# q and k made once per token group, attention scores for two heads at a time, identity products left out, and a new step order, in a one-core transformer kernel

## What is computed

```python
x = x + 0.5 * ffn(_layernorm(x))       # fp4-rounded FFN, inner width 352
x = x + mamba(_layernorm(x))           # 2 layers, 256 channels, 16 states each
x = x + 0.5 * ffn(_layernorm(x))
x = x + 0.5 * moe(_layernorm(x))       # 8 experts, hidden width 512
x = x + attn(_layernorm(x))            # 16 heads of 8, bias by distance, causal
x = x + 0.5 * moe(_layernorm(x))

# attn
xn = _layernorm(x, ln_gamma, ln_beta)
q = proj(Wq) / math.sqrt(DH); k = proj(Wk); v = proj(Wv)
scores = jnp.einsum('bhid,bhjd->bhij', q, k) + rel[:, dist]
attn = jax.nn.softmax(jnp.where(causal, scores, -inf), axis=-1)
return x0 + jnp.einsum('bhij,bhjd->bhid', attn, v).reshape(B, T, D) @ Wo.T
```

## Time and profile before

| | |
|---|---|
| median of 3 runs | 2702.1 us (2699.7 to 2704.14) |
| the profiled execution | 2699.89 us |
| its span from first to last instruction | 2698.1 us |
| mean granted TensorE clock | 0.969 of full |
| instructions | 41593 |

### The profile page before, as it was taken

One profiled execution on the slowest core, in us unless ns is written; L12 is line 12 of the kernel. 1 busy time (PEld: TensorE's weight loads), 2 busy tenths in 40 slices (PEclk: granted clock), 3 DMA queues, 4 the chain that ended last, 5 costly groups with the idle time before them and its releaser, 6 DMA issues.

```text
span 2698.1 us, 41593 instructions
## 1 busy us (share of the span) xinstructions
PE 2506.0 (93%) x14781; PEld 1756.5 (65%) x14781; DVE 1943.5 (72%) x3913; ACT 1612.1 (60%) x3465; POOL 1367.7 (51%) x1227
## 2 busy tenths in 40 slices
PE   7999999997898999887899999998999999999988
PEld 7888885785565655655555765756556656566665
DVE  5878798789787788687787688788787868532420
ACT  1424436443886567653776558664976786466754
POOL 1466474847373656456363745557373738321111
PEclk9999999998998999998999999998999999999989
DMA  4123121312121113112120212122120213000000
GB/s 153 52 75 102 46 90 48 94 56 71 42 85 32 56 47 96 45 58 63 47 80 33 78 41 63 48 67 63 40 87 29 79 41 94 17 5 1 1 5 5
DMA packets 88573, 150.59 MB, mean 56 GB/s; under 512 B 10565, under 2 KB 21485, under 8 KB 88110
## 3 DMA queue, kind: packets, MB, share of 16 engines
q1 hardware_dynamic: 88366, 147.94, 17.8%
HBM read 145.26 MB, written 2.65 MB: 55 GB/s over the span
## 4 chain that ended last, share of the span: by engine, by line
PE 75%; ACT 10%; DVE 8%; issue 4%; POOL 3%; DMA 0%; POOLq 0%; SPq 0%; DVEq 0%; ACTq 0%
PE c_bank L1369 16%; PE c_bank L924 15%; PE c_bank L916 14%; PE a_bank L762 7%; PE a_bank L752 3%; PE b_bank L1083 2%; DVE hst L710 2%; PE b_bank L1072 2%; PE a_bank L731 2%; PE b_bank L584 2%; ACT weighted_y L959 1%; DVE a_bank L704 1%; PE b_bank L565 1%; PE a_bank L768 1%; PE a_bank L736 1%
## 5 line engine op out<-in xcount | busy, mean ns | idle before, releaser
L833 POOL TENSOR_TENSOR prod_c<-hst,prod_c 128x512 f32<-128x512 f32 x512 | 666.3, 1307 | 411.1 <-DVE hst L710 384.0
L710 DVE TENSOR_TENSOR_SCAN hst<-dA,a_bank 128x512 f32<-128x512 f32 x512 | 621.8, 1214 | 14.8 <-ACT dA L822 4.5
L822 ACT ACTIVATE dA<-delta,a_neg 128x510 f32<-128x510 f32 x512 | 364.7, 719 | 320.5 <-DVE hst L710 314.8
L916 PE MATMUL c_bank<-c_xT,w 128*128 128x512 f32 x1024 | 532.4, 624 | 23.5 <-ACT weighted_y L959 11.8
L924 PEld LDWEIGHTS c_bank<-w,hid 128*128 128x128 f32 x4096 | 487.5, 192 | 57.9 <-ACT hid L951 26.8
L1369 PEld LDWEIGHTS c_bank<-ident 128*128 128x128 f32 x4004 | 484.6, 193 | 47.8 <-issue 39.3
L924 PE MATMUL c_bank<-w,hid 128*128 128x128 f32 x4096 | 511.1, 277 | 1.6 <-ACT hid L951 1.5
L1369 PE MATMUL c_bank<-ident 128*128 128x128 f32 x4004 | 491.8, 277 | 0.3 <-ACT weighted_y L959 0.3
L951 ACT ACTIVATE hid<-c_bank,b 128x512 f32<-128x512 f32 x512 | 349.1, 687 | 150.0 <-PE c_bank L916 147.4
L975 POOL TENSOR_TENSOR xs<-xs,weighted_y 128x512 f32<-128x512 f32 x128 | 167.5, 1309 | 497.3 <-ACT weighted_y L959 496.2
L704 DVE TENSOR_TENSOR a_bank<-du,a_bank 128x512 f32<-128x512 f32 x512 | 349.8, 683 | 72.6 <-PE a_bank L752 69.9
(11 more groups left out here) (182 smaller groups left out, 3159.8 us busy)
## 6 DMA issues: line engine op xcount, KB each, us to landing
prod_c<-c_rows SPq DMA_DIRECT2D x512, 256.0 KB, 3.2
w<-in_w SPq DMA_DIRECT2D x2, 2048.0 KB
xs<-in_x SPq DMA_DIRECT2D x8, 256.0 KB, 7.2
bias<-skew SPq DMA_DIRECT2D x1, 2048.0 KB, 8.4
out_dram<-xs SPq DMA_DIRECT2D x8, 256.0 KB, 2.3
in_wT<-in_in_wT SPq DMA_DIRECT2D x1, 512.0 KB
c_rows<-bcC SPq DMA_DIRECT2D x16, 32.0 KB, 1.6
b_hq<-in_w_gu SPq DMA_DIRECT2D x1, 384.0 KB, 3.3
```

What stands on the lines that cost most here:

```text
L710: nc.vector.tensor_tensor_scan(hst[:, s % RS, :], dA[:, s % RA, :], b_bank, 0.0, ALU.mult, ALU.add).then_inc(M.h.sem, 1)
L822: nc.scalar.activation(half_batches(dA[:, s % RA, :], 1), half_batches(delta[:, h, :], 1), ACT.Exp, scale=a_neg[:, l, h, n:n + 1]).then_in ...
L833: nc.gpsimd.tensor_tensor(prod[:, s % RP, :], hst[:, s % RS, :], cring[:, s % RC, :], ALU.mult).then_inc(M.pp.sem, 1)
L916: nc.tensor.matmul(S.bank[up_bank(e, c)][:, :], w1[:, e, c * 128:(c + 1) * 128], S.xT[:, :], start=True, stop=True).then_inc(M.up.sem, 1)
```

## The change

1. q and k. The weights have 128 columns each, in a permuted order (feature, head in group, group). PE makes one k product and one q product, ACT copies q once with its scale, DVE masks q and k and subtracts the high parts: four operations in all. SP writes high and low parts to a DRAM tensor `qk_rows`, six stores of 128 x 512, and reads them back as the strips, eight loads of 24 partitions x 4 rows (`b_sp`, a lane b on SP that did not exist). PE's first scores wait for these loads.
2. Scores. PE makes the scores of two heads in turn into banks 0 and 1, with one signal for both. The exponents' transposes move to bank 2, where the weighted values (columns 0 to 255) and their transposes (256 to 511) already are; `pr` has four buffers instead of three.
3. The 2002 identity products are gone: no letter d is left in `ORDER_PE`. `warm_pe` remains in the file and is never stepped.
4. All five order strings are written anew. One of them is shown; their rows say nothing without the steps they count.

```diff
 ORDER_SP = (
-    "a215c2a73caca64caca73ca62ca39c3")
+    "a165b4a62caca3b4a66c2a7b2a2b2a57c2b2ab2a65cb4a52baba3b2a10ca33b4cb4c2")
 
...
-        wqT = sb("wqT", [128, HG, 128])
-        wkT = sb("wkT", [128, HG, 128])
+        wqT = sb("wqT", [128, D])
+        wkT = sb("wkT", [128, D])
         wvT = sb("wvT", [128, D])
...
-        att_buf = sb("att_buf", [128, 2 * 384 + 3 * 384])
+        att_buf = sb("att_buf", [128, 2 * 384 + 4 * 384])
         sc = att_buf[:, 0:768].rearrange("p (b n) -> p b n", b=2)
-        pr = att_buf[:, 768:1920].rearrange("p (b n) -> p b n", b=3)
-        q_hi, q_all, k_hi = (att_buf[:, i * TOK:(i + 1) * TOK] for i in range(3))
+        pr = att_buf[:, 768:2304].rearrange("p (b n) -> p b n", b=4)
+        q_hi, k_hi, k_lo = (att_buf[:, i * TOK:(i + 1) * TOK] for i in range(3))
         nmx = sb("nmx", [128, 2, 2])
...
-        k_all = flat(sbb.xn[:, :, :])
+        q_lo = flat(sbb.xn[:, :, :])
...
-            for g in range(HG):
-                dve.wait_ge(M.qE.sem, L.at(M.qE, g + 1))
...
+            dve.wait_ge(M.qE.sem, L.at(M.qE, 1))
+            nc.vector.tensor_scalar(q_hi.bitcast(I32), q_lo.bitcast(I32), TOP12, None, ALU.bitwise_and).then_inc(M.qH.sem, 1)
+            yield
+            dve.wait_ge(M.k.sem, L.at(M.k, 1))
+            nc.vector.tensor_scalar(k_hi.bitcast(I32), S.bank[1][:, :].bitcast(I32), TOP12, None, ALU.bitwise_and).then_inc(M.kH.sem, 1)
+            yield
+            dve.wait_ge(M.qH.sem, L.at(M.qH, 1))
+            nc.vector.tensor_tensor(q_lo, q_lo, q_hi, ALU.subtract).then_inc(M.qS.sem, 1)
+            yield
+            dve.wait_ge(M.kH.sem, L.at(M.kH, 1))
+            nc.vector.tensor_tensor(k_lo, S.bank[1][:, :], k_hi, ALU.subtract).then_inc(M.kS.sem, 1)
+            yield
...
             for r in range(NH):
                 h = r % HEADS
-                dve.wait_ge(M.s.sem, L.at(M.s, r + 1))
+                dve.wait_ge(M.s.sem, L.at(M.s, r // 2 + 1))
                 if r >= 2:
                     dve.wait_ge(M.p.sem, L.at(M.p, r - 1))
                 for i, (c0, c1, b0) in enumerate(((0, 256, 0), (256, 384, 128))):
                     ins = nc.vector.tensor_tensor_reduce(
-                        out=sc[:, r % 2, c0:c1], in0=S.bank[0][:, c0:c1], in1=bias[:, h, b0:256], scale=1.0,
+                        out=sc[:, r % 2, c0:c1], in0=S.bank[r % 2][:, c0:c1], in1=bias[:, h, b0:256], scale=1.0,
                         scalar=-MASKED, op0=ALU.add, op1=ALU.min, accum_out=nmx[:, r % 2, i:i + 1])
                     if i:
                         ins.then_inc(M.m.sem, 1)
                     else:
                         ins.then_inc(L.sem, L.one())
                     yield
-                if r >= 9 and (r - 9) % 4 == 0:
-                    yield from y_end((r - 9) // 4)
-            for q in range((NH - 10) // 4 + 1, NH // 4):
-                yield from y_end(q)
+                if r >= 7 and r % 4 == 3:
+                    yield from y_end(r // 4 - 1)
+            yield from y_end(NH // 4 - 1)
...
-            for g in range(HG):
-                if g:
...
+            nc.tensor.matmul(S.bank[1][:, :], wkT[:, :], S.xT[:, :], start=True, stop=True).then_inc(M.k.sem, 1)
+            yield
+            nc.tensor.matmul(S.bank[0][:, :], wqT[:, :], S.xT[:, :], start=True, stop=True).then_inc(M.q.sem, 1)
+            yield
...
-            for r in range(NH + 4):
-                if r < NH:
...
+            def scores(r, queries, keys, part):
+
+                b, h = r // HEADS, r % HEADS
+                p0, s0 = 32 * (h % 4), b * SEQ
+                return nc.tensor.matmul(S.bank[r % 2][:, part], qT[p0:p0 + 3 * DH, h // 4, s0 + queries:s0 + queries + 128],
+                                        kT[p0:p0 + 3 * DH, h // 4, s0:s0 + keys], start=True, stop=True)
+
+            def exp_transposes(m):
+                pe.wait_ge(M.p.sem, L.at(M.p, m + 1))
+                if m:
+                    pe.wait_ge(M.pE.sem, L.at(M.pE, m))
+                if m and m % 4 == 0:
+                    pe.wait_ge(M.y.sem, L.at(M.y, m // 4))
+                for j in range(3):
+                    ins = nc.tensor.transpose(S.bank[2][:, j * 128:(j + 1) * 128], pr[:, m % 4, j * 128:(j + 1) * 128], ident[:, :])
+                ins.then_inc(M.pT.sem, 1)
+                yield
+
+            for w in range(NH // 2 + 2):
+                if w < NH // 2:
+                    if w == 0:
+                        pe.wait_ge(s_qk, 16 * 8 * (L.g + 1))
+                        pe.wait_ge(M.kS.sem, L.at(M.kS, 1))
                         pe.wait_ge(M.vE.sem, L.at(M.vE, 1))
-                    if r:
-                        pe.wait_ge(M.m.sem, L.at(M.m, r))
...
+                    if w:
+                        pe.wait_ge(M.m.sem, L.at(M.m, 2 * w))
+                    for r in (2 * w, 2 * w + 1):
+                        scores(r, 128, 256, slice(0, 256))
+                    scores(2 * w, 0, 128, slice(256, 384))
+                    scores(2 * w + 1, 0, 128, slice(256, 384)).then_inc(M.s.sem, 1)
+                    yield
+                if w >= 3 and w % 2:
+                    q = (w - 3) // 2
+                    pe.wait_ge(M.oE.sem, L.at(M.oE, q + 1))
+                    for t in range(2):
+                        ins = nc.tensor.transpose(S.bank[2][:, 256 + 128 * t:384 + 128 * t], oS[:, 128 * (1 - t):128 * (2 - t)], ident[:, :])
+                    ins.then_inc(M.oT.sem, 1)
+                    yield
+                if 1 <= w <= NH // 2:
+                    yield from exp_transposes(2 * w - 2)
+                    yield from exp_transposes(2 * w - 1)
+                if 2 <= w <= NH // 2 and w % 2 == 0:
+                    q = (w - 2) // 2
                     b = 4 * q // HEADS
                     pe.wait_ge(M.pE.sem, L.at(M.pE, 4 * q + 4))
-                    if q:
-                        pe.wait_ge(M.y.sem, L.at(M.y, q))
...
-                if r >= 7 and (r - 7) % 4 == 0:
-                    q = (r - 7) // 4
...
...
-            for g in range(HG):
-                act.wait_ge(M.q.sem, L.at(M.q, g + 1))
...
+            act.wait_ge(M.q.sem, L.at(M.q, 1))
+            nc.scalar.activation(q_lo, S.bank[0][:, :], ACT.Copy, scale=-float(DH ** -0.5)).then_inc(M.qE.sem, 1)
+            yield
+            for r in range(NH + 2):
                 if r < NH:
                     act.wait_ge(M.m.sem, L.at(M.m, r + 1))
-                    if r >= 3:
-                        act.wait_ge(M.pT.sem, L.at(M.pT, r - 2))
...
+                    if r >= 4:
+                        act.wait_ge(M.pT.sem, L.at(M.pT, r - 3))
+                    nc.scalar.activation(pr[:, r % 4, 0:256], sc[:, r % 2, 0:256], ACT.Exp, bias=nmx[:, r % 2, 0:1], scale=-1.0).then_inc(L.sem, L.one())
+                    yield
+                    nc.scalar.activation(pr[:, r % 4, 256:384], sc[:, r % 2, 256:384], ACT.Exp, bias=nmx[:, r % 2, 1:2], scale=-1.0).then_inc(M.p.sem, 1)
+                    yield
+                if r >= 2:
                     m = r - 2
                     act.wait_ge(M.pT.sem, L.at(M.pT, m + 1))
                     if m >= PT:
                         act.wait_ge(M.o.sem, L.at(M.o, (m - PT) // 4 + 1))
-                    nc.scalar.activation(pT[:, m % PT, :], S.bank[1][:, 0:384], ACT.Copy).then_inc(M.pE.sem, 1)
-                    yield
...
+                    nc.scalar.activation(pT[:, m % PT, :], S.bank[2][:, 0:384], ACT.Copy).then_inc(M.pE.sem, 1)
+                    yield
+                    if m % 4 == 3:
+                        q = m // 4
+                        act.wait_ge(M.o.sem, L.at(M.o, q + 1))
+                        if q:
+                            act.wait_ge(M.oT.sem, L.at(M.oT, q))
+                        nc.scalar.activation(oS[:, :], S.bank[2][:, 0:256], ACT.Copy).then_inc(M.oE.sem, 1)
+                        yield
...
+        def b_sp(sp, L):
+
+            for g in range(GROUPS):
+                L.g = g
+                rows = a["qk_rows"][g]
+                sp.wait_ge(att.qH.sem, L.at(att.qH, 1))
+                for p in (0, 1):
+                    sp.dma_start(rows[0, p], q_hi).then_inc(s_qkd, 16)
+                sp.wait_ge(att.kH.sem, L.at(att.kH, 1))
+                for p in (0, 2):
+                    sp.dma_start(rows[1, p], k_hi).then_inc(s_qkd, 16)
+                yield
+                sp.wait_ge(att.qS.sem, L.at(att.qS, 1))
+                sp.dma_start(rows[0, 2], q_lo).then_inc(s_qkd, 16)
+                sp.wait_ge(att.kS.sem, L.at(att.kS, 1))
+                sp.dma_start(rows[1, 1], k_lo).then_inc(s_qkd, 16)
+                yield
+                sp.wait_ge(s_qkd, 16 * 6 * (g + 1))
+                for i in range(2):
+                    strips = rows[i].rearrange("p (i j g) n -> (p i) j g n", i=DH, j=4)
+                    dst = qk[:, i, :, :].bitcast(F32)
+                    for j in range(4):
+                        sp.dma_start(dst[32 * j:32 * j + 3 * DH, :, :], strips[:, j, :, :]).then_inc(s_qk, 16)
```

(8 more changed lines are left out.)

231 lines of the change are left out of this document (74 added, 157 removed).

## The result

The changed kernel takes **2660.4 us** (median of 4 runs, 2659.3 to 2661.7) against 2703.1 for the kernel before on the same chip: a ratio of 0.984, 95% interval 0.983 to 0.986, so 1.6% faster. The forecast was 2654, with a range of 2588 to 2712. The profiled execution took 2661.7 us for a span of 2659.9.

A forecast was written before the change was run, and what follows sets the result against it. PE and VectorE together were taken to bound the middle, PE the end, and PE's work not the opening. Terms -66 - 5 - 25 + 43 + 5 = -48 us gave 2654 us; likeliest range 2615 to 2690, overall 2588 to 2712.

The forecast's parts named there:

- (c): Opening and middle: identity products hold real work back, so removing them gives -25 us (bounds -10 and -60).
- (d): Opening and middle: without identity products PE's granted clock falls, costing +43 us (bounds +15 and +95).
- Rival 2: Opening and layer boundaries: lower clock makes the kernel end slower, deciding from +91 us on, up to 2742 us; chance 0.19.
- (a): Attentions 0 to 5 beside mamba: removed PE and DVE work saves 11 us each, -66 us (bounds -30 to -84).
- The score pair: Attention scores on PE: two heads together save 0.21 to 0.58 us a pair; 4.5 us per attention taken.
- (b): End, attention 7 and the MoE beside it: -10 us of work, +15 uncovered, together -5 us (bounds -20 and +10).
- The thin stretch: End, before the last MoE: 10 to 15 us of thin PE, with nothing beside attention 7's last steps.
- (e): Attention's q and k trip through DRAM and back as strips: +5 us for eight attentions (bounds 0 and +60).
- The margin of 2.7 us: Attention 7: 16.5 us of PE work was to cover the strips' trip of 13.8 us.
- Rival 3: Attentions: strips come late, PE stands still 5 to 8 us per attention, 2690 to 2715 us; chance 0.07.
- The middle 60 to 80 us shorter: Mamba layers 5 to 15: this stage's span shrinks by 60 to 80 us, a sign for the forecast.
- if the new order leaves DVE waiting in the middle: Mamba layers 5 to 15: VectorE left waiting there would show the prediction wrong; no size given.

The follow-up runs named there:

- experiment 1: The kernel before without its 2002 unread identity products, nothing else touched: 2718.0 us, ratio 1.0058.
- experiment 2: The changed kernel with unread identity products put into PE's gaps: 2667.3 us with 1349 in the opening alone, 2661.4 us with 370 more behind 700 us.
- experiment 3: The changed kernel with a pair's four score products reordered, both of the first head, then both of the second: 2659.1 us, ratio 0.984.
- experiment 4: The changed kernel with each pair's score products split into two visits, one head each: 2738.9 us, ratio 1.014.
- experiment 8: The changed kernel with PE's and ScalarE's steps reordered behind 2489 us, attention 7 closer together and MoE passes wider apart: 2673.9 us, ratio 0.989.
- experiment 6: The changed kernel with each attention's eight strip loads made twice: 2739.3 us, ratio 1.014.
- the last version: The changed kernel with the kernel before's order and identity products up to 685 us, plus 370 identity products in PE's gaps behind 700 us: 2639.2 us, ratio 0.978.
- experiment 5: The changed kernel with spared work given back per attention: six PE products in one run, 2694.2 us; twelve VectorE operations in another, 2688.6 us.

## Why the prediction was right

By medians the way from 2701.4 to 2660.4 has three measured steps. Leaving out the identity products is +16.5 (experiment 1). From there to the changed kernel with the old opening, 2718.0 to 2652.2, is -65.8: the attention's work, the strips and the new order behind 640 us. The new order of the opening is +8.2. The prediction had +18, -71 with +5 for the strips, so -66, and no third step. That -66 and -65.8 agree so closely is luck, since the parts were off both ways.

- **Identity products and clock, (c) and (d).** The net was right, +18 for 16.5, both parts were too large. In the opening they were put at -15 and +28; the parts of experiment 1 show about -3 and +11 (the 11 is net of what the products held up in those stretches, which wasn't parted further). "Long stretches there will be at 0.50" was right, and more than half of the opening was at it (0.69 granted); what was oversized is "57 us if all of the opening ran at half clock". The prediction gave the clock no price in the end, where it fell from 0.98 to 0.90 and where the traces of experiment 2 differ by up to 7 us. Rival 2 began as it said, with the half clock from the start, but from 51.6 us on the clock went back and forth between the two levels, and its +91 was nowhere near.
- **The attention's work (a).** The sum of -66 came out, by parts that were not. The score pair saves 0.58 us, the upper bound, not 0.28, the one term of the sum that was clearly mis-sized. The row-group rule of the Trainium skill (TensorE: Matmul & The Clock Gate, Part 3, The mechanism) pointed to that bound, and this case's trace agrees with it: the second head's weight load starts 3 ns behind the first head's and runs beside its product, where one head's own second load starts 0.11 us behind its first product. The products of the two heads overlap too, and experiment 3 didn't end that; experiment 4 did, for most pairs. A pair at the upper bound should have made -66 larger, by 29 us over the six attentions; on the other side VectorE's waits for scores grew where 4 us less per attention were counted, and its work shows to three tenths in the middle, not in full. By layers the gain doesn't look like six equal attentions: the scans of layers 6, 8 and 10 are 26, 40 and 17 us shorter than before, those of layer 7 are 12 longer, and what lies outside the scans of layers 5 to 15 is 35 us longer in all. The written order and the work can't be parted further: the old order can't hold the new steps, so how much of the -65.8 is order stays open.
- **The end (b).** -5 forecast, -4 from MoE 12's start, and here the parts were right too. From MoE 13's start to MoE 14's, where attention 6 stands, 115.2 us became 107.1 (-10 forecast); from there to MoE 15's, with attention 7, 114.5 became 118.7 (+5 forecast). The thin stretch was 15 us of idle PE, as written. Experiment 8 shows one order that didn't take it away, and why.
- **The strips (e).** +5 forecast; PE waited 1.8, and what the late C rows of layer 10 cost isn't parted. The margin of 2.7 us came out at 1.4 in attention 7, by luck, since both its sides were wrong: the loads take 11.0 us until the last signal, not an issue train and one landing, 3.4 + 3.2; and the first scores come 22.7 us behind the start of the k product, not 16.5. Rival 3 was 1.4 us away; past that, each us costs one (experiment 6).
- **The step that was missing:** that the new order could be worse in a stage the attention doesn't touch. It is worth 8 us, about what lies between the forecast of -48 and the -41 measured.
- **"The middle 60 to 80 us shorter"** was met by 81, of which 21 are the mamba lane's lead; by the MoE marks it is 60, the edge of that range. The sign of being wrong "if the new order leaves DVE waiting in the middle" didn't show: it stands idle for 329 us there instead of 344.

## What to carry to other kernels

Where lanes advance by a written order, a stage's end must be read from every lane: a lane that runs ahead looks like a gain and is taken back, as in both the middle here and the last version. Idle filling that keeps a clock up is worth only what the real passes gain, less what it holds up: here 16.5 us for 492 us of busy PE, and 7 us lost when it was placed in the opening by gaps alone. Narrow products of two heads on different strips of partitions took PE the time of one head's, so heads should stand next to each other on a shared matmul engine; splitting 110 pairs cost more than the whole change had gained.

## What was not expected of the hardware

Four score products took 0.37 us where two did: the two heads' products start 3 to 7 ns apart, in either order of the program. Two visits cost 78.6 us where 64 were the most that 0.58 us for each explains.

The twelve VectorE operations of 128x512 that experiment 5 adds to each attention only read and write SBUF, the core's own memory, and they took 1.06 us in the mean, where the like of them (L979) takes 0.80. The mean hides two cases. The 29 that ran while GpSimd stood still took about 0.69 us, the 41 that ran nearly wholly beside GpSimd's work 1.31; L979 took 0.68 six times, and 1.15 and 1.16 the two times that GpSimd was at work.

A granted clock of 0.73 instead of 0.98 in an opening of 700 us cost 8 to 11 us, and one and the same order of steps was granted 0.98 in one execution and 0.92 in another.
